# Making du on GpSimd instead of VectorE in one of the two unit kinds of the state-space loop

## The chip, the cores and the metric

The kernel runs on one core of one Trainium2 chip. The metric is device time in microseconds for the whole batch of 16 sequences; lower is better.

## What is computed

Each of 16 sequences of 512 tokens by 128 channels goes through attention, a mixture of 8 experts, a selective state-space block and a second mixture. The change lies in the state-space block, which is solved as a fixed point: eight steps of the loop below and one more evaluation.

```python
def fp_step(y_prev):
    x_tilde = (x - y_prev) @ W_mix.T + y_prev                 # u in the kernel
    bc = _shift1(y_prev) @ W_bc.T
    Bt = bc_normalize(B0 + bc[..., :D_STATE])
    Ct = bc_normalize(C0 + bc[..., D_STATE:])
    y = _selective_scan(x_tilde, delta, A, Bt, Ct, D)
    return layer_norm(y)
# inside the scan, per token:
#   h = exp(dt * A) * h + (dt * u) * b        dt * u is du in the kernel
#   y = sum_n(h * c) + D * u
```

There are 256 channels with 16 states each, so 4096 scans of 512 tokens per step.

## The kernel before

**Tiling.** The 512 tokens are cut in two halves of 256 (`hf` 0 and 1). The 4096 scans of a half are 32 groups of 128 partitions, taken two at a time, so a unit of work is 16 slots `p` = 0 to 15, each 128 partitions by 512 elements. A unit of the second half (`hf` 1) starts its scans from the saved ends of the first half.

**The loop.** For each sequence there is a first unit, then 8 turns of two units, `scan_unit(turn, 1, ...)` on the second half and then `scan_unit(turn, 0, ...)` on the first half, and one last unit on the second half. That makes 128 turns and 256 loop units in all. While a unit scans one half, the same unit finishes the step of the other half (the steps called `back_`: sum, layer norm, new y) and prepares the other half's next step (the steps called `front_`: u, du, the normalised b and c, the copies of c, the first quarter of the scan inputs).

**The five queues of a unit.** Each engine runs its own list in program order, and semaphores alone join them.

- VectorE runs the 16 scans (L1606 for `hf` 0, two half scans each on L1616 for `hf` 1). Scan p waits for its input in PSUM and for product p-4 (four state buffers). Behind scan 3 come the moments of the other half's scan output (`back_var`, L1253), behind scan 4 `back_norm`, behind scan 6 `back_y` (L1591), behind scan 8 a small sum, and behind scan 11 first `front_du` (L1571, which reads u from PSUM) and then `front_norm` (L1532 to L1537).
- GpSimd runs the 16 products of the states with c (L1727), each behind its scan, and behind product 11 `skip` (L1700), u times D from the SBUF copy `u_sb`.
- TensorE brings the scan inputs to PSUM (L853), sums the products over the states two slots at a time (L843; the last two pairs of a unit are summed in the next unit, behind scan input 3), then adds the skip term (`back_d`, L817) and turns the sums (`back_z`, L825), which is what `back_var` waits for. u is made behind scan input 11 (`front_u`, L788) and the copies of c behind scan input 15 (L807), which wait for du, for the normalised c and for `u_sb`.
- ScalarE fills `scan_in` (L1127), copies the summed states (`back_sum`, L1143) behind half of the second quarter's fills, and at the end of a unit copies u to `u_sb` (`front_keep`, L1111), which waits for du; then come the first quarter's fills for the next unit, which wait for du and bcn, and the copy of c (L1119).
- SyncE stores scan ends.

Of the kernel before, what the change touches and what calls it, by code (L numbers as in the profile page):

```python
# [18 lines left out]
ALU = mybir.AluOpType  # L19
# [32 lines left out]
HB = TH // P  # L52
# [3 lines left out]

PE_Z, PE_X, PE_V, PE_BC, PE_U, PE_C = 3, 6, 6, 8, 11, 15
DVE_VAR, DVE_NORM, DVE_Y, DVE_BC, DVE_DU, DVE_BCN = 3, 4, 6, 8, 11, 11
POOL_SKIP = 11
AHEAD = 2  # L60
RESCORE = (3, 4)
QKV_BANK = (6, 2)
# [57 lines left out]
def hybrid_kernel(nc, t, out):  # L120

    with ExitStack() as ctx:
        sems = []

        def sb(name, shape, dt=F32):
            return ctx.enter_context(nc.sbuf_tensor(name, shape, dt))

        def signal(name, before=0, turn=0, behind=0, unit=1):
            s = Signal(ctx.enter_context(nc.semaphore(name)), before, turn, behind, unit)
            sems.append((name, s))  # L130
            return s
# [107 lines left out]
        u_sb = sb("u_sb", [P, HB, DI])  # L239
        x_bc = sb("x_bc", [P, TB, 2 * NS])  # L240
        cT = sb("cT", [NE, T])[:]
        delta = sb("delta", [P, TB, DI])
# [5 lines left out]
        du = sb("du", [P, 2, HB, DI])  # L248
# [101 lines left out]
        u_done = signal("u_done", *looped)  # L350
        du_done = signal("du_done", *once)
        sq_done = signal("sq_done", *once)
        u_copied = signal("u_copied", *looped)
        skip_done = signal("skip_done", *front)
# [623 lines left out]
        def _(eng):  # L978
# [128 lines left out]
                               ACT.Square).then_inc(sq_done.sem, sq_done.up(at))  # L1107

            def front_keep(at, hf, kf):
                eng.wait_ge(du_done.sem, du_done.count(at, kf + 1))  # L1110
                eng.activation(u_sb[:], half6, ACT.Copy).then_inc(u_copied.sem, u_copied.up(at))  # L1111

            def front_root(at, hf, kf):
# [100 lines left out]
            with eng.Fori(0, B) as b:  # L1214
                at = Place(b, 0)
# [14 lines left out]
                at = Place(b, 2)  # L1230
# [12 lines left out]
        def _(eng):  # L1243
# [316 lines left out]
            def front_bc(at, hf, kf):  # L1560

                eng.wait_ge(sq_done.sem, sq_done.count(at, kf + 1))
                eng.tensor_reduce(ss[:, 0:HB * 2], bcq[:, 0:HB].rearrange("p b k n -> p (b k) n"),
                                                 AX, ALU.add).then_inc(ss_done.sem, ss_done.up(at))
# [9 lines left out]
            def back_var(at, hf, kb, bank):  # L1574
                eng.wait_ge(z_done.sem, z_done.count(at, kb + 1))
                moments(at, half5, zvar, HB, to=z_moments(bank))

            def back_norm(at, hf, kb, bank):
                eng.wait_ge(zstd.sem, zstd.count(at, kb + 1))
                eng.reciprocal(rstd[:, 0:HB], std[:, 0:HB]).then_inc(vchain.sem, vchain.up(at))  # L1580
                eng.wait_ge(vchain.sem, vchain.last(at))
                eng.scalar_tensor_tensor(
                    out=nmr[:, 0:HB], in0=z_moments(bank)[:, :, 0], scalar=-1.0, in1=rstd[:, 0:HB],
                    op0=ALU.mult, op1=ALU.mult).then_inc(znmr.sem, znmr.up(at))
# [11 lines left out]
            def scan_unit(at, hf, ks, kb, kf):  # L1596

                other = 1 - hf
                for p in range(NP):
                    eng.wait_ge(b_done.sem, b_done.count(at, NP * ks + p + 1))  # L1600
                    eng.wait_ge(prod_done.sem, prod_done.count(at, NP * ks + p - NHID + 1))
                    end = ended[p % NHID]
                    if hf == 0:
                        if p >= NHID:
                            eng.wait_ge(end.sem, end.count(at, p // NHID))
                        eng.tensor_tensor_scan(  # L1606
                            hst[:, p % NHID, :],
                            da[:, 0, 2 * p:2 * p + 2, :].rearrange("p s t -> p (s t)"),
                            bank(RING[p % 4]), 0.0, ALU.mult, ALU.add
                            ).then_inc(scanned.sem, scanned.up(at))  # L1610
                    else:
                        if p < NHID:
                            eng.wait_ge(end.sem, end.count(at, 0))
                        for s in range(2):
                            half = slice(s * TH, (s + 1) * TH)
                            ins = eng.tensor_tensor_scan(  # L1616
                                hst[:, p % NHID, half], da[:, 1, 2 * p + s, :],
                                ps[:, RING[p % 4], half], hend[:, 2 * p + s:2 * p + s + 1],
                                ALU.mult, ALU.add)
                        ins.then_inc(scanned.sem, scanned.up(at))  # L1620
                    if p == DVE_VAR:
                        back_var(at, other, kb, 7)
                    if p == DVE_NORM:
                        back_norm(at, other, kb, 7)
                    if p == DVE_Y and kf is not None:
                        back_y(at, other, kb)
                    if kf is not None:
                        if p == DVE_BC:
                            front_bc(at, other, kf)
                        if p == DVE_DU:  # L1630
                            front_du(at, other, kf)
                        if p == DVE_BCN:
                            front_norm(at, other, kf)

            def ssm_output(at):
# [36 lines left out]
            with eng.Fori(0, B) as b:  # L1672
                at = Place(b, 0)
# [10 lines left out]
                at = Place(b, 2)  # L1684
# [9 lines left out]

        @block.gpsimd
        def _(eng):
            def skip(at, hf, kf):

                eng.wait_ge(u_copied.sem, u_copied.count(at, kf + 1))
                eng.tensor_tensor(  # L1700
                    skip_u[:, hf], u_sb[:],
                    w["skip"][:].rearrange("p (o c) -> p o c", o=1).broadcast_to([P, HB, DI]),
                    ALU.mult).then_inc(skip_done.sem, skip_done.up(at))

            def first_unit(at):

                eng.wait_ge(stored.sem, stored.count(at, 1))
                for p, (m, j) in enumerate(FIRST):
                    eng.wait_ge(scanned.sem, scanned.count(at, p + 1))
                    if p == 0:  # L1710
                        eng.wait_ge(c_copied.sem, c_copied.count(at, 1))
                    if p >= 8:

                        last = max(q for q in range(p) if FIRST_PROD[q] == FIRST_PROD[p])
                        k = FIRST_SUMS.index(2 * FIRST[last][0] + FIRST[last][1] // 2)
                        eng.wait_ge(nsummed.sem, nsummed.count(at, k + 1))
                    product(at, 0, p, m, FIRST_PROD[p])
                for hf in range(2):
                    eng.wait_ge(x_mixed_a.sem, x_mixed_a.count(at, 1))
                    eng.tensor_tensor(  # L1720
                        skip_u[:, hf], x_mixed[:, hf * HB:(hf + 1) * HB, :],
                        w["skip"][:].rearrange("p (o c) -> p o c", o=1).broadcast_to([P, HB, DI]),
                        ALU.mult).then_inc(skip_done.sem, skip_done.up(at))

            def product(at, hf, p, m, to):

                eng.tensor_tensor(  # L1727
                    prod[:, to, :].rearrange("p (s t) -> p s t", s=2),
                    hst[:, p % NHID, :].rearrange("p (s t) -> p s t", s=2),
                    crep[:, hf, m, :].rearrange("p (o t) -> p o t", o=1).broadcast_to([P, 2, TH]),  # L1730
                    ALU.mult).then_inc(prod_done.sem, prod_done.up(at))

            def scan_unit(at, hf, ks, ready, kf):

                for p in range(NP):
                    eng.wait_ge(scanned.sem, scanned.count(at, NP * ks + p + 1))
                    if p == 0:
                        eng.wait_ge(c_copied.sem, c_copied.count(at, ready))
                    if p % BATCH == 0:
                        eng.wait_ge(nsummed.sem, nsummed.count(  # L1740
                            at, NB * ks + (p - PROD) // BATCH + 1 + LAG))
                    product(at, hf, p, p // QP, p % PROD)
                    if p == POOL_SKIP and kf is not None:
                        skip(at, 1 - hf, kf)

            eng.wait_ge(loaded, 16 * n_loads)
            with eng.Fori(0, B) as b:
                at = Place(b, 0)
                first_unit(at)
                with eng.Fori(0, ITERS) as i:  # L1750
                    turn = Place(b, 1, i)
                    scan_unit(turn, 1, 0, 0, 0)
                    scan_unit(turn, 0, 1, 1, 1)
                scan_unit(Place(b, 2), 1, 0, 0, None)
# [54 lines left out]
```

## Time and profile before

| | before |
|---|---|
| median of 3 runs | 10247.87 us (10247.55 to 10253.49) |
| profiled execution | 10245.85 us, its span 10243.8 us |
| VectorE busy | 8689.7 us, 85% |
| ScalarE busy | 7120.1 us, 70% |
| GpSimd busy | 6123.1 us, 60% |
| TensorE busy (matmul / weight load) | 9253.0 us, 90% / 6324.7 us, 62% |

Shares are over the whole span, which also holds the attention and the mixtures, in which GpSimd does nothing. Busy matmul time holds matmuls that overlap. In the loop the trace has to be read by stretch: a turn takes some 46 us and repeats 128 times, so 0.1 us in each turn is 12.8 us of the total.

### The profile page before, as it was taken

What the parts mean: (1) busy time and instruction counts of PE and PEld (TensorE: products, weight loads), DVE (VectorE), ACT (ScalarE), POOL (GpSimd) and SP (SyncE); (2) the same over time, 40 slices, a digit from 0 to 9 for tenths busy, and PEclk for the clock granted to TensorE, in tenths of its full rate; (3) what the DMA queues carried; (4) which work ended last, traced back from release to release, by engine and by line L of the source; (5) the groups of instructions that cost most, each with busy time, mean ns of one, the idle gap of its engine ahead of it and who ended that gap; (6) DMA issues with size and microseconds to landing.
All of it is one profiled execution on the core that took longest, in us unless ns stands there. A gap on an engine that the chain in (4) does not pass through costs nothing.

```text
span 10243.8 us, 255404 instructions
## 1 busy us (share of the span) xinstructions
PE 9253.0 (90%) x86610; PEld 6324.7 (62%) x86610; DVE 8689.7 (85%) x16668; ACT 7120.1 (70%) x14939; POOL 6123.1 (60%) x4900
## 2 busy tenths in 40 slices
PE   7999899998999989999899999999899999999988
PEld 4656656566565665656656566565665656656566
DVE  6978979789797897978979799797997979879698
ACT  5867758677685776857768576685766858668586
POOL 1936829368293772937729277392773927739286
PEclk9999999999999999999999999999999999999999
DMA  1010000000000000000000000000000000100000
GB/s 39 1 21 1 5 17 0 21 1 5 17 0 21 1 5 17 0 21 1 7 15 0 21 1 10 12 0 21 1 14 8 0 21 1 17 4 0 21 1 3
DMA packets 690794, 95.17 MB, mean 9 GB/s; under 512 B 633594, under 2 KB 684989, under 8 KB 685245
## 3 DMA queue, kind: packets, MB, share of 16 engines
q1 hardware_dynamic: 690237, 88.00, 6.6%
q8 instruction: 318, 5.21, 0.2%
q14 instruction: 239, 1.96, 0.1%
HBM read 60.26 MB, written 25.22 MB: 8 GB/s over the span
## 4 chain that ended last, share of the span: by engine, by line
PE 29%; DVE 25%; POOL 17%; issue 16%; ACT 10%; DVEq 1%; POOLq 1%; DMA 1%; SPq 0%; ACTq 0%
POOL work L1727 16%; DVE work L1616 10%; DVE work L1606 6%; PE ps L644 5%; ACT scan_in L1127 4%; PE ps L634 4%; PE ps L629 3%; PE ps L532 3%; PE ps L555 3%; PE ps L567 2%; ACT yscT L1160 1%; DVE stats L1253 1%; DVE scan_in L1520 1%; POOL skip_u L1700 1%; ACT ytmp L1148 1%
## 5 line engine op out<-in xcount | busy, mean ns | idle before, releaser
L1727 POOL TENSOR_TENSOR work<-work,crep 128x512 f32<-128x512 f32 x4608 | 5770.9, 1279 | 4050.1 <-DVE work L1555 3540.3
L1127 ACT ACTIVATE scan_in<-du,bcn 128x256 f32<-128x256 f32 x8832 | 3693.2, 499 | 79.4 <-PE ps L853 46.4
L1616 DVE TENSOR_TENSOR_SCAN work<-da,hend,ps 128x256 f32<-128x256 f32 x4608 | 3029.1, 726 | 64.3 <-PE ps L853 51.6
L853 PE MATMUL ps<-w_ident,scan_in 128*128 128x128 f32 x18432 | 2465.7, 279 | 286.2 <-ACT scan_in L1127 150.0
L853 PEld LDWEIGHTS ps<-w_ident,scan_in 128*128 128x128 f32 x18432 | 2026.8, 142 | 892.8 <-issue 331.3
L1606 DVE TENSOR_TENSOR_SCAN work<-da,ps 128x512 f32<-128x512 f32 x2048 | 2353.8, 1201 | 38.7
L843 PE MATMUL ps<-work,w_sel 128*32 128x256 f32 x17792 | 1413.8, 391 | 277.2 <-POOL work L1727 277.2
L1048 ACT ACTIVATE work<-ps,w_gate_b 128x512 f32<-128x512 f32 x512 | 351.5, 687 | 809.5 <-PE ps L629 752.8
L843 PEld LDWEIGHTS ps<-work,w_sel 128*32 128x32 f32 x17792 | 375.8, 108 | 756.3 <-POOL work L1727 535.2
L1346 DVE TENSOR_REDUCE smax<-ps 128x1 f32<-128x512 f32 x1024 | 642.8, 684 | 136.5 <-PE ps L532 128.6
L1014 ACT ACTIVATE da<-ps 128x512 f32<-128x512 f32 x1024 | 585.6, 598 | 184.1 <-PE ps L555 168.1
L1446 DVE SCALAR_TENSOR_TENSOR work<-ps,w_up_b,work 128x512 f32<-128x512 f32 x512 | 378.1, 749 | 302.1 <-PE ps L634 287.0
L1111 ACT ACTIVATE u_sb<-ps 128x512 f32<-128x512 f32 x256 | 153.2, 598 | 607.8 <-DVE du L1571 607.8
L807 PE MATMUL ps<-w_ident,bcn 128*32 128x128 f32 x18432 | 574.5, 278 | 0.0
L807 PEld LDWEIGHTS ps<-w_ident,bcn 128*32 128x32 f32 x18432 | 514.2, 112 | 89.1 <-ACT u_sb L1111 59.9
L634 PE MATMUL ps<-xnT,up_w 128*128 128x512 f32 x1024 | 526.2, 595 | 23.3 <-DVE work L1446 23.3
L644 PEld LDWEIGHTS ps<-down_w,work 128*128 128x128 f32 x4096 | 488.7, 192 | 88.0 <-issue 80.3
L629 PE MATMUL ps<-xnT,gate_w 128*128 128x512 f32 x1024 | 526.0, 595 | 0.0
L532 PE MATMUL ps<-da 96*128 96x512 bf16 x1024 | 441.2, 438 | 77.0 <-issue 45.2
L644 PE MATMUL ps<-down_w,work 128*128 128x128 f32 x4096 | 496.8, 276 | 0.0
L788 PE MATMUL ps<-mix_y,yT 128*128 128x256 f32 x2048 | 484.4, 379 | 0.0
L1455 DVE SCALAR_TENSOR_TENSOR work<-ps,rt,work 128x128 f32<-128x128 f32 x960 | 269.8, 343 | 196.3 <-PE ps L644 196.3
(201 smaller groups left out, 11716.6 us busy)
## 6 DMA issues: line engine op xcount, KB each, us to landing
da<-parts_d SPq DMA_DIRECT2D x192, 192.0 KB
hend<-work SPq DMA_DIRECT2D x2304, 1.0 KB, 1.8
parts_d<-scan_in SPq DMA_DIRECT2D x80, 256.0 KB, 2.5
da<-pad_d SPq DMA_DIRECT2D x32, 208.0 KB
da<-pad_d SPq DMA_DIRECT2D x32, 192.0 KB
x_in<-in_x SPq DMA_DIRECT2D x17, 256.0 KB, 2.8
out<-work SPq DMA_DIRECT2D x16, 256.0 KB
gate_w<-in_gate_w SPq DMA_DIRECT2D x1, 1024.0 KB, 4.9
```

The source lines that it names most:

```text
L532: mm = eng.matmul(bank(u % 3), q[:, qb * P:(qb + 1) * P], k, start=True, stop=True)
L629: mm = eng.matmul(bank(u % 2), gate_w[:, e, f * P:(f + 1) * P], xnT[:], start=True, stop=True)
L634: mm = eng.matmul(bank(2 + u % 2), up_w[:, e, f * P:(f + 1) * P], xnT[:], start=True, stop=True)
L644: mm = eng.matmul(blocks(6 + e % 2)[:, tb, :], hid[:, e % 2, f, tb * P:(tb + 1) * P], down_w[:, e, f, :], start=(tb == 0 and f == 0), stop ...
L807: mm = eng.matmul(ps[GC * k:GC * (k + 1), bank + m // 2, c:c + P], bcn[:, hf, tb, 1, n:n + 1].broadcast_to([P, GC]), ident[:], start=(m % ...
L843: mm = eng.matmul(ps[GC * q:GC * (q + 1), 3, j % 2 * TH:(j % 2 + 1) * TH], w["sel"][:], prod[:, p % PROD, q % 2 * TH:(q % 2 + 1) * TH], st ...
L853: mm = eng.transpose(ps[:, bank, c:c + P], scan_in[:, m, tb, 2 * j + s].rearrange("p k c -> p (k c)"), ident[:])
L1127: ins = eng.activation(scan_in[:, m, tb, :, k, :], du[:, hf, tb, :].rearrange("p (e c) -> p e c", c=GC), ACT.Copy, scale=bcn[:, hf, tb, 0, ...
L1346: eng.tensor_reduce(smax[:, h % 2, qb:qb + 1], bank(u % 3), AX, ALU.max).then_inc(maxed.sem, maxed.up(at))
L1606: eng.tensor_tensor_scan(hst[:, p % NHID, :], da[:, 0, 2 * p:2 * p + 2, :].rearrange("p s t -> p (s t)"), bank(RING[p % 4]), 0.0, ALU.mult ...
L1616: ins = eng.tensor_tensor_scan(hst[:, p % NHID, half], da[:, 1, 2 * p + s, :], ps[:, RING[p % 4], half], hend[:, 2 * p + s:2 * p + s + 1], ...
L1727: eng.tensor_tensor(prod[:, to, :].rearrange("p (s t) -> p s t", s=2), hst[:, p % NHID, :].rearrange("p (s t) -> p s t", s=2), crep[:, hf, ...
```

## The change

In the units of the second half, which prepare half 0, du is no longer made by VectorE. ScalarE copies u to `u_sb` as soon as TensorE has made it (and the earlier skip has read the old copy), and GpSimd makes du from `u_sb` behind product 9. VectorE's `front_norm` goes from behind scan 11 to behind scan 10 in these units. In the units of the first half nothing changes.

```diff
-POOL_SKIP = 11
+POOL_DU, POOL_SKIP, DVE_BCN_1 = 9, 11, 10
@@ scalar
             def front_keep(at, hf, kf):
-                eng.wait_ge(du_done.sem, du_done.count(at, kf + 1))
+                if hf == 1:
+                    eng.wait_ge(du_done.sem, du_done.count(at, kf + 1))
+                else:
+                    eng.wait_ge(u_done.sem, u_done.count(at, kf + 1))
+                    eng.wait_ge(skip_done.sem, skip_done.count(at, kf))
                 eng.activation(u_sb[:], half6, ACT.Copy).then_inc(u_copied.sem, u_copied.up(at))
@@ vector
-                        if p == DVE_DU:
+                        if p == DVE_DU and hf == 0:
                             front_du(at, other, kf)
-                        if p == DVE_BCN:
+                        if p == (DVE_BCN_1 if hf else DVE_BCN):
                             front_norm(at, other, kf)
@@ gpsimd
+            def front_du(at, hf, kf):
+
+                eng.wait_ge(u_copied.sem, u_copied.count(at, kf + 1))
+                eng.tensor_tensor(du[:, hf], u_sb[:], delta[:, hf * HB:(hf + 1) * HB, :],
+                                  ALU.mult).then_inc(du_done.sem, du_done.up(at))
@@ gpsimd scan_unit
                     product(at, hf, p, p // QP, p % PROD)
+                    if p == POOL_DU and hf == 1 and kf is not None:
+                        front_du(at, 0, kf)
                     if p == POOL_SKIP and kf is not None:
                         skip(at, 1 - hf, kf)
```

## Rows read from the trace of the kernel before

**Rows 1.** The page, part 1: busy time and share of the span by engine.

```profile
PE 9253.0 (90%) x86610; PEld 6324.7 (62%) x86610; DVE 8689.7 (85%) x16668; ACT 7120.1 (70%) x14939; POOL 6123.1 (60%) x4900
```

**Rows 2.** Busy time by window: stretch, length, busy us of PE, PEld, DVE, ACT, POOL.

```profile
320.57:333.65 13.08, 11.42 (x103) 7.90 (x101) 12.69 (x27) 12.94 (x28) 10.94 (x9) 1.00 0.02 0
333.65:346.57 12.92, 11.56 (x150) 8.45 (x149) 12.85 (x23) 8.55 (x21) 12.58 (x11) 1.00 0.00 0
```

**Rows 3.** Timeline of VectorE: start us, length us, engine, line, operation.

```profile
331.40 0.88 DVE L1591 SCALAR_TENSOR_TENSOR yT<-ps,gamma_s,ytmp 128x256 f32<-128x256 f32 x2 [0.23 <-PE ps L834]
...
334.88 3.93 DVE L1616 TENSOR_TENSOR_SCAN work<-da,hend,ps 128x256 f32<-128x256 f32 x6
338.72 0.67 DVE L1571 TENSOR_TENSOR du<-ps,delta 128x512 f32<-128x512 f32 x1
339.30 0.15 DVE L1532 TENSOR_SCALAR rn<-ps 128x4 f32<-128x4 f32 x1
...
339.92 5.21 DVE L1616 TENSOR_TENSOR_SCAN work<-da,hend,ps 128x256 f32<-128x256 f32 x8
...
349.49 0.74 DVE L1253 BATCH_NORM_STATS2 stats<-ps 128x6 f32<-128x256 f32 x2
...
350.62 1.22 DVE L1606 TENSOR_TENSOR_SCAN work<-da,ps 128x512 f32<-128x512 f32 x1
```

**Rows 4.** Timeline of GpSimd, runs of alike instructions merged.

```profile
333.65 6.59 POOL L1727 TENSOR_TENSOR work<-work,crep 128x512 f32<-128x512 f32 x5 [1.00 <-DVE work L1616]
340.20 1.28 POOL L1700 TENSOR_TENSOR skip_u<-u_sb,w_skip 128x512 f32<-128x512 f32 x1
341.50 10.04 POOL L1727 TENSOR_TENSOR work<-work,crep 128x512 f32<-128x512 f32 x8
352.04 1.27 POOL L1727 TENSOR_TENSOR work<-work,crep 128x512 f32<-128x512 f32 x1 [0.49 <-DVE work L1606]
```

**Rows 5.** Timeline of GpSimd in narrow windows: products 9, 10 and 15 alone.

```profile
336.33 1.27 POOL L1727 TENSOR_TENSOR work<-work,crep 128x512 f32<-128x512 f32 x1
...
337.72 1.28 POOL L1727 TENSOR_TENSOR work<-work,crep 128x512 f32<-128x512 f32 x1
...
345.29 1.28 POOL L1727 TENSOR_TENSOR work<-work,crep 128x512 f32<-128x512 f32 x1
```

**Rows 6.** Timeline of ScalarE.

```profile
335.10 1.70 ACT L1127 ACTIVATE scan_in<-du,bcn 128x256 f32<-128x256 f32 x4
339.42 0.60 ACT L1111 ACTIVATE u_sb<-ps 128x512 f32<-128x512 f32 x1 [2.62 <-DVE du L1571]
340.13 3.30 ACT L1127 ACTIVATE scan_in<-du,bcn 128x256 f32<-128x256 f32 x8
...
347.33 0.60 ACT L1143 ACTIVATE yscT<-ps 128x512 f32<-128x512 f32 x1 [1.39 <-PE ps L843]
347.83 1.70 ACT L1127 ACTIVATE scan_in<-du,bcn 128x256 f32<-128x256 f32 x4
```

**Rows 7.** Timeline of TensorE's matmuls.

```profile
330.62 0.66 PE L834 MATMUL ps<-w_ident,yscT 128*128 128x128 f32 x4 [0.53 <-ACT yscT L1160]
...
334.97 1.89 PE L788 MATMUL ps<-mix_y,yT 128*128 128x256 f32 x8
...
346.63 0.64 PE L843 MATMUL ps<-work,w_sel 128*32 128x256 f32 x8 [0.21 <-POOL work L1727]
...
348.17 1.05 PE L825 MATMUL ps<-w_ident,yscT 128*128 128x128 f32 x8
...
349.72 1.53 PE L853 MATMUL ps<-w_ident,scan_in 128*128 128x128 f32 x12
```

**Rows 8.** Waits of VectorE over the whole run: us in total, times, longest.

```profile
DVE stats L1253 <- PE ps L825: 48.4, 16, 3.4
```

**Rows 9.** Timeline at a sequence's end: L825 and the moments that waited.

```profile
622.72 1.05 PE L825 MATMUL ps<-w_ident,yscT 128*128 128x128 f32 x8
...
623.81 0.76 DVE L1253 BATCH_NORM_STATS2 stats<-ps 128x6 f32<-128x256 f32 x2 [1.17 <-PE ps L825]
```

## The prediction

> **What bounds the kernel now.** I started at the page's busy shares [rows 1] and put them aside, because over the whole span GpSimd looks like the idle engine (60%), and that is an average with stages where it has nothing to do. The change touches only the loop, so I read one turn: the unit of the second half from 320.57 to 345.05 us, and the unit of the first half behind it. Two views matter, busy time by window and the timelines of the single engines.
>
> VectorE sets the pace for most of it. In the stretch from product 7 to product 15 it is busy 12.85 of 12.92 us [rows 2]. But GpSimd is busy 12.58 us of the same 12.92, in the second of the two rows [rows 2], while its spare time lies ahead of that: 10.94 busy of the 13.08 us before. The reader is to see that GpSimd has 2.1 us to spare in the first half of the unit and 0.34 us in the second, and the change puts its work into the second. The timeline says the same: five products run 333.65 to 340.24 almost back to back, the skip starts at 340.20 as they end, and eight more products follow from 341.50 without a gap that is listed [rows 4]. The last four of those eight belong to the next unit, so product 15 of this unit is the one at 345.29 [rows 5].
>
> Now who waits for product 15. TensorE's sum of it starts at 346.63 and had waited for GpSimd [rows 7]; ScalarE's copy of the sums starts at 347.33, and had waited 1.39 us for TensorE [rows 6]; the turn of the sums runs 348.17 to 349.22 [rows 7]; and VectorE's moments start at 349.49 [rows 3]. So product 15 ends at 346.57, the moments' input is ready 2.65 us later, and the moments run 0.27 us after that. They don't wait today: all the waiting of the moments for L825 over the whole run is 16 waits, one per sequence [rows 8], none in a loop unit. VectorE arrives just behind its input. That thin slack decides the change: how soon a ready turn lets the moments go is seen at a sequence's end, where they start 0.04 us after its last matmul ends (623.77 to 623.81) [rows 9]; at another pair of the two engines it is 0.12 us (331.28 to 331.40) [rows 3, 7]. The real slack is therefore 0.15 to 0.23 us.
>
> **The change, part by part.**
>
> *VectorE loses du.* From its start at 338.72 to the next instruction's start at 339.30 it is 0.58 us [rows 3]. One per turn, 128 turns: 74 us, if VectorE is what the turn waits for.
>
> *front_norm goes one scan up.* The same instructions, 0.62 us (339.30 to 339.92) [rows 3], now ahead of scan 11 instead of behind it. Scan 11 then ends 0.6 us later than before, at about 339.4, and all behind it 0.58 us earlier. Product 11 will start after 340.1 (below), so nothing on GpSimd waits for it. TensorE's input 15 reuses scan 11's bank and slips by up to 0.6 us, and the copies of c behind it too; ScalarE's copy of c today follows fills that end at 343.43 [rows 6], so it does not come late. Cost nothing; the cover is those fills.
>
> *ScalarE's copy of u moves up.* u's matmuls end at 336.86 [rows 7], ScalarE's fills at 336.80 [rows 6]. ScalarE follows TensorE by 0.06 us (347.27 to 347.33) [rows 6, 7], so the copy starts at 336.92 instead of 339.42 and, at 0.60 us, ends at 337.52. The new wait for the old skip is met a unit ago. Queued behind the copy are the first quarter's fills, which need du: see next.
>
> *GpSimd gains du behind product 9.* Product 9 ends at 337.60, with the next one at 337.72 today [rows 5]. Such instructions follow each other every 1.24 us when nothing holds them (337.72 to the skip at 340.20 is two) [rows 4, 5]. The new du is not in the trace; the nearest rows are the products and the skip, of the same 128x512 shape, 1.24 us apart at the least and 1.30 from the skip to product 12 at the most (340.20 to 341.50) [rows 4]. I take 1.24, since the 1.30 ends in a product that also needs its scan. Its start lies between 337.55 (back to back, instructions overlap by 0.04) and 337.72 (the copy's end at 337.52 plus the 0.20 us that a product needs behind a scan, 351.84 to 352.04) [rows 3, 4]; I take 337.67. Product 10 then starts at 337.67 + 1.24 = 338.91 instead of 337.72, which is 1.19 late; from the ends 1.07 to 1.31.
>
> From there six steps lead to product 15 (11, skip, 12, 13, 14, 15), 1.24 apart: 338.91 + 6 x 1.24 = 346.35, against 345.29 today. That is 1.06 late; a little of the 1.19 is won back, because today the steps take 7.57 us for 7.44 of work, and now a backlog fills the holes. With no winning back it is up to 1.31; with all of it and the early start, 0.94.
>
> *The fills.* du ends at about 338.95 (337.67 + 1.28) and bcn is made before scan 11, so the fills start about 1.1 us before today's 340.13 [rows 6]. The next unit's first input is early: no cost, and no gain, since today scan 0 of the next unit does not wait.
>
> *The moments.* L825 ends at 349.22 + 1.06 = 350.28, the moments start 0.04 us later at 350.32, against 349.49 today. VectorE reaches that point 0.58 us sooner and stands idle 1.4 us: the 0.58 saved and 0.83 more. From the ends: 0.94 - 0.27 + 0.04 = 0.71 and 1.31 - 0.27 + 0.12 = 1.16.
>
> *Behind the moments.* GpSimd's product 3 of the next unit ends at 351.54 + 1.06 = 352.60; product 4 follows its scan, today at 352.04 [rows 4] and then at 352.87. So GpSimd has caught up, by its idle 0.49 us there and by VectorE's delay, and the rest of the turn runs as before, only later. TensorE's input for scan 4 starts 1.06 late too, at 350.78, and its first four matmuls need some 0.5 us [rows 7]; scan 4 wants it at 350.62 + 0.83 = 351.45 [rows 3]. This just fits.
>
> **The sum.** 128 turns x 0.83 = 106 us. On the profiled execution's 10245.85 us (a span of 10243.8 us and 2 us around it, which stay) that is 10352; the median of the runs stands 2 us higher than the profiled execution, so 10354. The bounds give 128 x 0.71 = 91 and 128 x 1.16 = 148: 10339 to 10396.
>
> **The rivals.**
>
> *Faster: VectorE remains the bound.* If GpSimd could take in du's 1.24 us before product 15, the turn would lose 0.58 us: 10248 - 74 = 10174. The point from which it decides is the shift of product 15: the turn gets shorter only where that shift is under 0.23 us, and the full win needs product 15 to come 0.35 us sooner than today (0.23 - 0.58). Against it stands that only 0.34 us are idle in the stretch [rows 2] and 1.24 are added. For it stands the 85% of VectorE, and that VectorE is the busiest engine in the loop. The Trainium skill, "Perfetto Trace Analysis", section "Optimizing Scalar/DVE Operations", speaks for this rival: with a saturated VectorE it may make sense to move work to ScalarE or GpSimd. The chain from product 15 speaks against it here. Chance 7%.
>
> *Within 0.2%.* A shift of product 15 of only 0.1 to 0.4 us (the slack of 0.23 us and 20 us over 128 turns, 0.16 us, on either side), if the pace of 1.24 were set by the scans and not by GpSimd, so that a backlog would run off faster. Against it: the eight products from 341.50 keep the same pace across the change to the faster scans of the next unit, 10.04 us for eight [rows 4]. Chance 3%: 10228 to 10268.
>
> *Slower by more: the fills lose the last 0.1 us.* Behind the sum of product 15, ScalarE's four fills (347.83 to 349.53) [rows 6] release the input of scan 4. They are 1.06 late where the moments are 0.83 late, and if the input comes 0.2 us late as well, or the root of the variance does, the turn costs 1.06 to 1.3 us: 10248 + 136 to 166 = 10384 to 10414. Chance 10%.
>
> *Contention.* While GpSimd runs products back to back, VectorE's half scans take 3.93 us for six and 5.21 us for eight, 0.65 each [rows 3]: they are not held up, and a du in place of a product reads no more than that. Were VectorE held for du's whole 1.24 us, it would lie in the idle 1.4 us ahead of the moments and move the forecast by nothing. By the Trainium skill, "SBUF — State Buffer", section "Who interferes with whom", a VectorE instruction with two SBUF inputs contends with a GpSimd instruction that reads SBUF, and one with a single SBUF input does not; the scans read one operand from PSUM, and the trace agrees. That would matter in the faster rival alone, whose 0.58 us it could take away.
>
> **Chances and range.** Forecast 80%, faster rival 7%, same 3%, more costly rival 10%. About 0.2% (20 us) is what a measurement can tell from no change. Faster 0.07, same 0.03, slower 0.90. The range takes in the bounds of the unknown costs and a little of the costlier rival: 10330 to 10400.
>
> **What would show each step.** VectorE: a wait of the moments (L1253) for L825 in every unit of the first half, about 1.4 us, some 180 us in all where 48 stand now, and VectorE's busy time down by about 74 us. GpSimd: du starting 17.1 us after the unit's first scan, and product 15 ending 27.1 us after it against 26.0 now. The unit of the second half (first scan to first scan) shorter by 0.58 us, the one of the first half longer by 1.4. ScalarE's copy of u 2.5 us earlier. The prediction is wrong if the moments don't wait, or if GpSimd shows more room between products 9 and 15 than 0.34 us, or if du on GpSimd takes clearly other than 1.24 us.

## The result and the profile after

The changed kernel takes 10436.09 us, median of 4 runs (10434.82 to 10437.35), against 10247.71 us before: a ratio of 1.0184 (95% interval 1.0167 to 1.02), 188 us slower. The forecast was 10354 us, its range 10330 to 10400 us. The sign was right, and the size was not: 188 us where 106 were forecast.

The page of the changed kernel, part 1. VectorE's busy time fell by 63 us and GpSimd's rose by 135 us against [rows 1]:

```profile
span 10434.0 us, 255532 instructions
PE 9292.3 (89%) x86610; PEld 6363.1 (61%) x86610; DVE 8627.0 (83%) x16540; ACT 7130.0 (68%) x14939; POOL 6257.6 (60%) x5028
```

Waits of VectorE and of GpSimd over the whole run of the changed kernel (us in total, times, longest). The moments now wait in every unit of the first half, as forecast; but 128 new waits of the forecast 1.4 us would give some 180 us, and the total rose by 242 us from [rows 8], with waits of 2.9 us that no step of the sum explains. GpSimd also waits for TensorE's sums: 32 of these waits stood before (23 us in all), and 64 of some 2 us are new, in the long turns that follow here:

```profile
DVE stats L1257 <- PE ps L825: 290.1, 144, 2.9
...
POOL work L1737 <- PE ps L843: 151.0, 96, 2.1
```

Two turns of VectorE's timeline in the changed kernel, the unit of the first half of one turn and then all of the next. The answers to [rows 3] are the scans, the moments (L1257) and scan 4:

```profile
301.97 4.53 DVE L1610 TENSOR_TENSOR_SCAN work<-da,ps 128x512 f32<-128x512 f32 x4
309.38 0.76 DVE L1257 BATCH_NORM_STATS2 stats<-ps 128x6 f32<-128x256 f32 x2 [2.89 <-PE ps L825]
...
310.67 1.22 DVE L1610 TENSOR_TENSOR_SCAN work<-da,ps 128x512 f32<-128x512 f32 x1 [0.23 <-PE ps L853]
...
326.76 5.21 DVE L1620 TENSOR_TENSOR_SCAN work<-da,hend,ps 128x256 f32<-128x256 f32 x8
...
350.62 4.53 DVE L1610 TENSOR_TENSOR_SCAN work<-da,ps 128x512 f32<-128x512 f32 x4
356.40 0.76 DVE L1257 BATCH_NORM_STATS2 stats<-ps 128x6 f32<-128x256 f32 x2 [1.25 <-PE ps L825]
...
357.69 1.22 DVE L1610 TENSOR_TENSOR_SCAN work<-da,ps 128x512 f32<-128x512 f32 x1 [0.23 <-PE ps L853]
...
373.78 1.38 DVE L1620 TENSOR_TENSOR_SCAN work<-da,hend,ps 128x256 f32<-128x256 f32 x2
```

The turn from 326.76 to 373.78 takes 47.02 us, 0.9 more than the 46.1 before. That is close to the forecast of 0.83 more. In the turn ahead of it the same moments waited 2.89 us instead of 1.25. The two kinds alternate nearly throughout: over the run 64 of the 128 units of the first half take 24.7 us (24.59 to 24.82) and 64 take 23.16 us (23.08 to 23.19), where all took 21.65 before.

TensorE's matmuls in the same two places of the changed kernel, from the sum of products 12 and 13 on. The short wait's turn stands second:

```profile
302.69 0.64 PE L843 MATMUL ps<-work,w_sel 128*32 128x256 f32 x8
305.12 1.06 PE L843 MATMUL ps<-work,w_sel 128*32 128x256 f32 x8 [1.79 <-POOL work L1737]
306.11 2.08 PE L817 MATMUL ps<-skip_u,w_ident 128*128 128x256 f32 x4
307.98 1.36 PE L825 MATMUL ps<-w_ident,yscT 128*128 128x128 f32 x8
...
351.35 0.64 PE L843 MATMUL ps<-work,w_sel 128*32 128x256 f32 x8
353.78 0.64 PE L843 MATMUL ps<-work,w_sel 128*32 128x256 f32 x8 [1.79 <-POOL work L1737]
354.35 1.13 PE L817 MATMUL ps<-skip_u,w_ident 128*128 128x256 f32 x4
355.31 1.05 PE L825 MATMUL ps<-w_ident,yscT 128*128 128x128 f32 x8
```

The order is the same, and so is TensorE's idle time ahead of the sum, 1.79 us. But four matmuls of L817 take 2.08 us in one place and 1.13 in the other, and the sum 1.06 against 0.64. The granted clock says why. Busy time by window in the changed kernel (after the busy times, the granted clock as a share of 2.4 GHz, DMA share and GB/s):

```profile
302.00:304.00 2.00, 1.23 (x12) 0.58 (x12) 2.00 (x3) 0.65 (x2) 2.00 (x3) 1.00 0.00 0
304.00:306.00 2.00, 0.88 (x8) 0.18 (x8) 2.00 (x3) 0.00 (x0) 2.00 (x2) 0.80 0.15 1
306.00:308.00 2.00, 2.00 (x9) 1.53 (x6) 0.49 (x1) 1.77 (x5) 2.00 (x3) 0.50 0.15 1
308.00:310.00 2.00, 2.00 (x18) 1.47 (x17) 0.62 (x2) 1.22 (x4) 1.99 (x2) 0.85 0.00 0
...
352.00:354.00 2.00, 0.22 (x4) 0.16 (x8) 2.00 (x3) 0.00 (x0) 2.00 (x3) 1.00 0.07 1
354.00:356.00 2.00, 2.00 (x19) 1.55 (x12) 1.16 (x2) 1.52 (x4) 2.00 (x2) 1.00 0.15 1
```

In the long turn the clock falls to 1.2 GHz (0.50) as TensorE's wait for product 15 ends: here 0.08 us behind the sum's start, over the 64 long turns between 0.32 us ahead of it and 0.92 us behind it. Most of the chain of matmuls to the moments runs at it. From product 15's end, 0.05 us ahead of the sum, to the end of L825 it is 4.3 us (305.07 to 309.34) instead of 2.6 (353.73 to 356.36). The Trainium skill, "TensorE: Matmul & The Clock Gate", section "Part 1: The HAM clock gate", says that a gate sets TensorE's clock to one of these two levels by how busy the engine has lately been; the trace agrees, with 0.50 behind the wait and 1.00 elsewhere in the loop.

GpSimd of the changed kernel in the later turn, the answer to [rows 4, 5]:

```profile
343.82 1.27 POOL L1704 TENSOR_TENSOR du<-u_sb,delta 128x512 f32<-128x512 f32 x1
345.05 2.52 POOL L1737 TENSOR_TENSOR work<-work,crep 128x512 f32<-128x512 f32 x2
347.52 1.30 POOL L1710 TENSOR_TENSOR skip_u<-u_sb,w_skip 128x512 f32<-128x512 f32 x1
348.76 9.90 POOL L1737 TENSOR_TENSOR work<-work,crep 128x512 f32<-128x512 f32 x8
```

du starts 17.06 us after the unit's first scan (17.1 was forecast) and the next product 1.23 us behind it. Everything from there to the end of the eight products is one backlog.

### The profile page after: what moved, and what is told of

The parts are those of the page before. It is cut to its first block, busy times and chain, and to the rows that moved or that the text cites. A ratio compares the mean times of both kernels' runs of the same rounds, so it can differ in the third digit from the quotient of the medians.

```text
span 10434.0 us, 255532 instructions
## 1 busy us (share of the span) xinstructions
PE 9292.3 (89%) x86610; PEld 6363.1 (61%) x86610; DVE 8627.0 (83%) x16540; ACT 7130.0 (68%) x14939; POOL 6257.6 (60%) x5028
## 4 chain that ended last, share of the span: by engine, by line
PE 35%; POOL 22%; DVE 21%; issue 13%; DMA 4%; ACT 2%; POOLq 1%; DVEq 1%; SPq 0%; ACTq 0%
POOL work L1737 21%; DVE work L1610 8%; DVE work L1620 6%; PE ps L644 4%; DMA hend<-work 4%; PE ps L634 4%; PE ps L853 3%; PE ps L629 3%; PE ps L532 3%; PE ps L555 3%; PE ps L567 2%; PE ps L817 2%; PE ps L843 2%; PE ps L825 1%; DVE stats L1257 1%
## 5 line engine op out<-in xcount | busy, mean ns | idle before, releaser
L843 PE MATMUL ps<-work,w_sel 128*32 128x256 f32 x17792 | 1438.2, 397 | 452.7 <-POOL work L1737 449.0
L1147 ACT ACTIVATE yscT<-ps 128x512 f32<-128x512 f32 x288 | 171.6, 596 | 482.0 <-PE ps L843 470.6
L1257 DVE BATCH_NORM_STATS2 stats<-ps 128x6 f32<-128x256 f32 x576 | 215.8, 416 | 290.1 <-PE ps L825 290.1
```

Source lines behind the costliest of these rows:

```text
L843: mm = eng.matmul(ps[GC * q:GC * (q + 1), 3, j % 2 * TH:(j % 2 + 1) * TH], w["sel"][:], prod[:, p % PROD, q % 2 * TH:(q % 2 + 1) * TH], st ...
```

## The experiments

Each ran beside the kernel before on the same chip; ratios are to that kernel, whose median was 10256.96 us beside the first four experiments and 10247.58 us beside the last three.

**TensorE kept busy while it waits.** The changed kernel, and:

```diff
                     for k in range(LAG):
                         if p == LATE_AT[k]:
+                            if k == LAG - 1 and hf == 0:
+                                eng.wait_ge(c_copied.sem, c_copied.count(at, kf))
+                                keep_busy(10, 6)
                             sum_states(at, ks - 1, NB - LAG + k)
```

> The changed kernel, with ten spare transposes on TensorE in the units of the first half, between the sums of products 12, 13 and of 14, 15, where TensorE now waits 1.79 us for GpSimd. Theory (half of the loss is TensorE's clock, which is granted at half in every second turn right behind that wait): the clock stays up, the moments wait 1.25 us in all turns instead of 2.8 us in 64 of them, 10436 - 64 x 1.55 = about 10337 us. Rival (the 2.8 us are GpSimd's own backlog, which alternates): no change, 10436 us. If the transposes are too many and delay the sum, each 0.13 us of that costs 17 us.

Measured: 10334.85 us, ratio 1.0078 (1.0062 to 1.0095), with 1280 transposes more than the changed kernel. Its timeline, TensorE and then VectorE, in a unit of the first half:

```profile
350.31 0.64 PE L843 MATMUL ps<-work,w_sel 128*32 128x256 f32 x8 [0.58 <-POOL work L1740]
350.88 1.13 PE L817 MATMUL ps<-skip_u,w_ident 128*128 128x256 f32 x4
351.85 1.05 PE L825 MATMUL ps<-w_ident,yscT 128*128 128x128 f32 x8
...
352.94 0.76 DVE L1260 BATCH_NORM_STATS2 stats<-ps 128x6 f32<-128x256 f32 x2 [1.28 <-PE ps L825]
```

TensorE still waits for GpSimd, but 0.58 us at a stretch; the clock stays up in all 128 turns, and the moments wait 1.23 to 1.31 us in every one. The turn is 47.01 us. Work that computes nothing took about 1% off the changed kernel's time, so the clock was worth that much. The rival, GpSimd's own alternating backlog, falls.

**A spare GpSimd product in two places.** The kernel before, VectorE keeping its du, with one unused product of the same shape. N is 9 in one kernel and 6 in the other:

```diff
                     product(at, hf, p, p // QP, p % PROD)
+                    if p == N and hf == 1 and kf is not None:
+                        eng.tensor_tensor(x_in[:].rearrange("p b c -> p (b c)").rearrange("p (b c) -> p b c", b=HB),
+                                          x_mixed[:, 0:HB, :], delta[:, 0:HB, :], ALU.mult)
```

> The kernel before, VectorE still making du, with one more GpSimd product of du's size behind product 9 in the units of the second half, its output unused. Theory (the chain from product 15 to the moments, with VectorE's saving worth nothing): the turn gets longer by the 0.8 to 0.9 us of the forecast, 10350 to 10363 us; TensorE waits only about 1.3 us for product 15, not 1.8, since VectorE is not ahead, so whether the clock also falls is open; if it falls as in the changed kernel, about 10450. Rival (the loss comes from the order of waits on u, ScalarE's early copy or the later du): 10248 us, or well under 10340.

> The same extra GpSimd product as in the kernel with it behind product 9, but behind product 6. Theory (only GpSimd's work between product 7 and product 15 costs; the 1.0 us of idle time ahead of product 7 takes this one in): 10248 us, at most 10260. Rival (GpSimd's total load or a contention with VectorE costs): 10350 us or more, as with the other place.

Measured: behind product 9, 10350.82 us, ratio 1.0096 (1.0079 to 1.0113); behind product 6, 10256.14 us, ratio 1.0001 (0.9991 to 1.0011). GpSimd's timeline with the product behind product 6, the spare one on L1744:

```profile
286.40 2.68 POOL L1727 TENSOR_TENSOR work<-work,crep 128x512 f32<-128x512 f32 x2 [0.42 <-DVE work L1616]
289.03 1.30 POOL L1744 TENSOR_TENSOR x_in<-x_mixed,delta 128x512 f32<-128x512 f32 x1
290.26 6.39 POOL L1727 TENSOR_TENSOR work<-work,crep 128x512 f32<-128x512 f32 x5
```

The 1.0 us of idle time ahead of product 7 [rows 4] is gone, the rest is made up in the next five products (6.39 us, against 6.59), and the turn keeps its 46.10 us. The same 1.24 us three products later cost 0.86 us per turn, 46.96 us. So neither GpSimd's load nor a contention with VectorE is the price, but the place.

The kernel with the spare product behind product 9, TensorE and VectorE at the start of a unit of the first half:

```profile
303.13 0.64 PE L843 MATMUL ps<-work,w_sel 128*32 128x256 f32 x8 [1.15 <-POOL work L1727]
...
305.76 0.76 DVE L1253 BATCH_NORM_STATS2 stats<-ps 128x6 f32<-128x256 f32 x2 [0.62 <-PE ps L825]
```

TensorE waits 1.12 to 1.18 us in every turn, and the clock does not fall in any of the 128. In this kernel VectorE has nothing taken off it, and it is 0.9% faster than the changed one.

**VectorE's du taken off, GpSimd given nothing.** The kernel before, with one column of each block made in the units of the second half (the rest of du keeps old values, so this kernel leaves out work that the result needs):

```diff
+                if hf == 0:
+                    eng.tensor_tensor(du[:, 0, :, 0:1], half6[:, :, 0:1], delta[:, 0:HB, 0:1],
+                                      ALU.mult).then_inc(du_done.sem, du_done.up(at))
+                    return
```

> The kernel before, VectorE making only one column of each block of du in the units of the second half, GpSimd given nothing: du of the first half stays stale, so the result is not the reference's. It prices VectorE's time alone. Theory (the moments' input, set by GpSimd's product 15, comes only 0.15 to 0.23 us before they run, and GpSimd wins back at most 0.14 us): 0.3 to 0.4 us per turn, 10248 - 38 to 51 = 10197 to 10210 us, with the moments now waiting. Rival (VectorE is the bound): the whole 0.5 us per turn, 10184 us.

Measured: 10216.07 us, ratio 0.9961 (0.9947 to 0.9975), so 0.39% or 40 us, where the chain's theory had 38 to 51 us and the full saving would be 64. The turn is 0.24 us shorter, a little less than the 0.3 to 0.4 expected. The unit of the second half is 0.55 us shorter and the one of the first half 0.31 us longer (means over the 128 turns). What takes the 0.31 us back:

```profile
299.97 0.64 PE L843 MATMUL ps<-work,w_sel 128*32 128x256 f32 x8 [0.59 <-POOL work L1731]
...
302.60 0.76 DVE L1253 BATCH_NORM_STATS2 stats<-ps 128x6 f32<-128x256 f32 x2
...
303.89 1.22 DVE L1610 TENSOR_TENSOR_SCAN work<-da,ps 128x512 f32<-128x512 f32 x1 [0.23 <-PE ps L853]
```

The moments start 0.14 us later after the unit's first scan than before (4.58 against 4.45 us), and scan 4 starts another 0.17 us later behind them (1.29 against 1.12 us), having waited 0.23 us for its input, which is also late behind product 15's sum. That second wait stands in every kernel here whose moments follow L825 at once (0.04 us behind it), the changed one included, and the forecast's sum had put it at nothing.

**VectorE given its time back.** The changed kernel, GpSimd making du, and VectorE one unused product of du's shape behind scan 10, where `front_norm` now stands:

```diff
+                        if p == DVE_DU - 1 and hf == 1:
+                            eng.tensor_tensor(x_in[:].rearrange("p b c -> p (b c)").rearrange("p (b c) -> p b c", b=HB),
+                                              half5, delta[:, 0:HB, :], ALU.mult)
```

> The changed kernel, GpSimd making du, and VectorE given back a product of du's size behind scan 10 (PSUM and SBUF in, output unused), so that it gains no time. Theory (VectorE's 0.58 us go into waiting for product 15's sum, and by letting TensorE finish its other work sooner they stretch its wait from about 1.15 to 1.79 us, behind which the clock falls): with more work the kernel gets faster, about 10350 us, TensorE waiting about 1.15 us for product 15, its clock at full in the loop. Rival (the clock falls for another reason of this kernel, the order of the front steps): 10436 us.

Measured: 10347.0 us, ratio 1.0096 (1.0079 to 1.0113). TensorE and VectorE of this kernel:

```profile
303.65 0.64 PE L843 MATMUL ps<-work,w_sel 128*32 128x256 f32 x8 [1.21 <-POOL work L1740]
...
306.28 0.76 DVE L1257 BATCH_NORM_STATS2 stats<-ps 128x6 f32<-128x256 f32 x2 [0.67 <-PE ps L825]
```

Giving VectorE 0.58 us of useless work in each turn made the changed kernel about 0.9% faster. TensorE waits 1.2 us (1.19 to 1.22 over the 128 turns) instead of 1.79, since the scans that it must see before it can sum products 12 and 13 end later, and its clock does not fall in the loop. This shows the cause from the other side: the change's own saving made the idle stretch long enough.

**The skips moved out of the way.** GpSimd's two skip products go behind product 6 of the next unit, where [rows 4] shows 1.0 us of idle time ahead of product 7. They are needed only two units later. In the first kernel this is added to the change, in the second to the kernel before. The core of both:

```diff
-        u_copied = signal("u_copied", *looped)
-        skip_done = signal("skip_done", *front)
+        u_copied = signal("u_copied", *once)
+        skip_done = signal("skip_done", 1, 2, 1)
...
-                    if p == POOL_SKIP and kf is not None:
-                        skip(at, 1 - hf, kf)
+                    if p == POOL_SKIP:
+                        skip(at, hf, 1 - hf)
...
+                eng.wait_ge(skip_done.sem, skip_done.count(at, kf + 1))
                 eng.activation(u_sb[:], half6, ACT.Copy).then_inc(u_copied.sem, u_copied.up(at))
```

> The changed kernel with both skip products moved from behind product 11 to behind product 6 of the next unit, where GpSimd waits for scans (the first unit leaves half 1's to the loop, ScalarE copying x_mixed to u_sb for it). Theory (GpSimd's work between product 7 and product 15 is what counts, VectorE's saving helps only as far as the chain from product 15 lets it): product 15 ends 0.15 us sooner than before the change, the moments wait about 0.2 us, the turn is 0.25 to 0.4 us shorter: 10248 - 32 to 51 = 10197 to 10216 us, TensorE's wait at 0.7 us and no fall of its clock. Rival (GpSimd's total load): no better than 10330 us. Rival (VectorE alone): 10174 us.

> The kernel before with both skip products moved to behind product 6 of the next unit and du left to VectorE. Theory (VectorE paces the turn as long as GpSimd's tail is no longer than today's): product 15 ends 1.2 us sooner and nothing follows from it, 10240 to 10255 us, at most 0.15 us per turn from scan 4's input, which waits today (10229). Rival (the chain from product 15 bounds the kernel before too): 10200 us or less.

Measured: with GpSimd's du, 10186.5 us, ratio 0.9936 (0.992 to 0.9953), 61 to 66 us faster than the kernel before and 2.4% faster than the changed one. Without it, 10217.49 us, ratio 0.9973 (0.9963 to 0.9983). The first kernel's TensorE and VectorE:

```profile
303.14 0.64 PE L843 MATMUL ps<-work,w_sel 128*32 128x256 f32 x8 [0.59 <-POOL work L1740]
...
305.77 0.76 DVE L1260 BATCH_NORM_STATS2 stats<-ps 128x6 f32<-128x256 f32 x2
...
307.06 1.22 DVE L1613 TENSOR_TENSOR_SCAN work<-da,ps 128x512 f32<-128x512 f32 x1 [0.23 <-PE ps L853]
```

GpSimd's total work is the same as in the changed kernel, and the loss is a gain. Both kernels did better than expected, and by the same 0.2 us per turn in the unit of the second half (24.25 against 24.45 us in the second kernel). In the kernel before, VectorE waits there 0.23 us for L834 [rows 3]. Over the run those waits, before and then in the kernel with the skips alone moved (the view lists idle stretches of 0.15 us and more):

```profile
DVE yT L1591 <- PE ps L834: 26.0, 112, 0.2
```

```profile
DVE yT L1595 <- PE ps L834: 3.5, 23, 0.2
```

Most of those waits did not go but fell below what the view lists: from 0.23 to 0.14 us in a turn. The rest is made up ahead of them. The first scan of the unit and ScalarE's copy of the sums, before:

```profile
320.57 5.21 DVE L1616 TENSOR_TENSOR_SCAN work<-da,hend,ps 128x256 f32<-128x256 f32 x8
323.50 0.60 ACT L1143 ACTIVATE yscT<-ps 128x512 f32<-128x512 f32 x1
```

The same with the skips alone moved, with GpSimd's products 12 to 15 of the unit ahead and four of this unit at the front and the step that waits for L834 at the end:

```profile
320.20 9.90 POOL L1731 TENSOR_TENSOR work<-work,crep 128x512 f32<-128x512 f32 x8 [0.25 <-DVE work L1610]
323.27 5.21 DVE L1620 TENSOR_TENSOR_SCAN work<-da,hend,ps 128x256 f32<-128x256 f32 x8
326.00 0.58 ACT L1147 ACTIVATE yscT<-ps 128x512 f32<-128x512 f32 x1
333.88 0.88 DVE L1595 SCALAR_TENSOR_TENSOR yT<-ps,gamma_s,ytmp 128x256 f32<-128x256 f32 x2
```

So the kernel before was held a little by GpSimd in its other unit as well. Without the skip in front, product 15 of the first half's unit ends 1.91 instead of 2.17 us after the next unit's first scan. That is 0.26 us sooner and not 1.2, since product 12 now waits for its scan. ScalarE's copy of the sums starts 0.2 us sooner (2.73 against 2.93 us), and with it all that ScalarE has behind it; VectorE takes the root of the variance 0.1 us sooner and the step behind L834 0.2 us sooner (10.61 against 10.83 us). In the unit of the second half the missing skip changed nothing: product 15 ends 1.51 us after the next unit's first scan in both kernels, right behind its own scan. So in the kernel before VectorE and GpSimd reach that point level, and GpSimd has nothing to give. The expectation was wrong in both its parts, the 1.2 us of product 15 and that nothing follows, and by 30 us in the time.

## Why the prediction was wrong

*The place and the chain: right.* GpSimd's 12.58 of 12.92 us [rows 2] and the chain from product 15 through the sum, the copy and L825 decide. The same 1.24 us behind product 6 cost nothing and behind product 9 cost 0.86 us per turn; the forecast for the whole change was 0.83.

*Product 15 1.06 us late: 0.98 us.* Over the 128 turns it ends 26.95 us after the unit's first scan instead of 25.97. The copy, du's start and its 1.24 us were right within 0.05 us.

*The moments 0.83 us late: 0.73 us in the turns with the full clock,* the 0.1 less mostly of product 15.

*Scan 4 "just fits": wrong by 0.17 us.* Its input comes late, scan 4 waits 0.23 us, and it starts 1.29 us behind the moments instead of 1.12. The turn at full clock is 0.90 us longer (47.00 us; 47.01 with TensorE kept busy), 115 us in 128 turns.

*VectorE's 74 us worth nothing here: right, and worse.* The unit of the second half got 0.61 us shorter, where 0.58 were forecast (VectorE's busy time fell by 63 us and not by 74), and all of it went into waiting. TensorE cannot sum products 12 and 13 before it has brought in scan input 3, which needs the last scan of the unit before. With VectorE 0.6 us ahead and GpSimd 1.0 behind, TensorE's wait for product 15 went from 0.21 [rows 7] to 1.79 us.

*The chain's 2.65 us taken as fixed: this is the step that failed.* The prediction moved the matmuls from product 15 to L825 by 1.06 us and left their length. I never costed TensorE's own wait, only VectorE's. In 64 of the 128 turns the clock fell to 1.2 GHz at the end of that wait, the chain took 4.3 us instead of 2.6, and the turn 1.55 us more (24.71 against 23.16 us): 64 x 1.55 = 99 us (the 64 stretches of half clock are all the loop has, and the kernel before has none there). Keeping TensorE busy or shortening its wait to 1.2 us took this away.

*The sum with these terms.* 115 + 99 = 214 us, which is what was measured in the loop (128 turns of 47.78 instead of 46.10 us on average). The span grew by 190 us: outside the loop the changed kernel is 24 us faster. There the stretches of half clock, summed over the trace's clock records, fell from 564 to 471 us, and the kernel with TensorE kept busy shows the same (468 us, and 23 us off), while the others, with 547 to 585 us, are within 6 us of before outside the loop. Executions of one and the same kernel differ alike: of the fourteen of the kernel before beside the first four experiments, the one with the highest mean granted clock, 0.973, took 10240.5 us, and the one with the lowest, 0.967, took 10268.65 us. That the clock is the cause of the 24 us is argued from this, not shown; whether the change moved those stretches, and how, is open.

*The rivals.* The faster rival asked for 1.24 us of room before product 15, and the kernel with the skips moved shows what happens once most of it is there: faster by 0.6%, though the unit of the first half is still 0.31 us longer than before, and 0.2 us of the gain per turn come from the other unit. The costlier rival had the late fills, 0.17 us of it true, and no clock. Of contention nothing was seen: 1.24 us of a product with two SBUF inputs in GpSimd's idle time left the time as it was (ratio 1.0001).

What decides that only half of the turns, nearly every second one, lose their clock, with the same 1.79 us of idle time in both, these runs do not settle.

## What to carry to other kernels

Read an engine's room in the stretch between its last idle gap and the instruction that others wait for, not over the span or even the unit: here the same 1.24 us were free in one place and cost 0.86 us three instructions later. When a step moves, cost the idle time that it makes on every engine of the chain, TensorE above all: a longer wait there can lower its clock and stretch the matmuls behind it. And if taking work from the busiest engine brings nothing, look for what can leave the queue of the engine that it waits for; moving two products that nobody needed for two units brought 0.3% alone, and turned the du's loss of 1.8% into a gain of 0.6%.

## What was unexpected of the hardware

TensorE, otherwise busy in the loop, kept its clock through waits of 0.2, 0.6, 1.15 and 1.2 us ahead of the sum, and lost it around the end of 64 of the 128 waits of 1.79 us (1.71 to 1.81); matmuls of L817 then took 2.08 us instead of 1.13 for four. Adding useless work made the kernel faster twice, by about 1% on TensorE and about 0.9% on VectorE.
